# 4-bit feed-forward: two constants leave the vector engine's passes, and two quantisations are interleaved except for groups 0, 1 and 7

## The reference, cut to what matters

```
def fp4_quant_dequant(x):                      # BLOCK = 16
    xb = x.reshape(shape[:-1] + (shape[-1] // BLOCK, BLOCK))
    scale = jnp.maximum(jnp.max(jnp.abs(xb), axis=-1, keepdims=True) / 6.0, 1e-12)
    xn = xb / scale
    idx = jnp.searchsorted(_MID, jnp.abs(xn))
    q = _GRID[idx] * jnp.sign(xn) * scale
    return q.reshape(shape)
def fp4_linear(x, w):
    return jnp.einsum('bsk,nk->bsn', fp4_quant_dequant(x), fp4_quant_dequant(w))

gate = fp4_linear(x, w_gate)                   # 128 -> 352
y = fp4_linear(x, w_up)                        # 128 -> 352
h = silu(gate) * y
return fp4_linear(h, w_down)                   # 352 -> 128
...
x = x + 0.5 * _L3_ffn_ref(_layernorm(x, axis=-1), ...)      # layer 10 and layer 12
```

## Time and profile before

| | |
|---|---|
| median of 3 runs | 4637.05 us (4632.97 to 4646.21) |
| the profiled execution's own time | 4633.54 us |
| its span, first to last instruction | 4631.7 us |
| busy over the span | PE 86%, DVE 75%, ACT 66%, POOL 33% |
| granted TensorE clock, mean | 0.925 of full speed |
| first 4-bit stage | about 3547 to 3729 us of the span |
| second 4-bit stage | about 4438 us to the end |

### The profile page before, as it was taken

How to read it: one execution, slowest core, us unless ns; L and a number is a source line. 1 busy time by engine, 2 the same in 40 slices (tenths; PEclk the granted TensorE clock), 3 DMA queues, 4 the chain that set the end, 5 groups by cost and what they waited for, 6 DMA issues and landing times.

```text
span 4631.7 us, 66074 instructions
## 1 busy us (share of the span) xinstructions
PE 3976.3 (86%) x15980; PEld 2217.0 (48%) x15980; DVE 3491.4 (75%) x11277; ACT 3068.7 (66%) x5649; POOL 1524.9 (33%) x2846
## 2 busy tenths in 40 slices
PE   5688759999999999999999999984978659999965
PEld 4466624444444444444444444432555437676644
DVE  6888489888788788787887887866657946665578
ACT  3455239999899899898998999971222226555532
POOL 2222134444444444444444444433000023333310
PEclk8788779999999999999999999996998779999987
DMA  2122010000000000000000000000000001111100
GB/s 56 28 40 30 15 23 1 8 17 1 20 5 1 22 3 8 17 1 20 5 1 22 3 13 12 1 1 0 1 0 0 0 28 42 41 39 36 40 1 18
DMA packets 148935, 71.87 MB, mean 16 GB/s; under 512 B 109241, under 2 KB 141710, under 8 KB 146212
## 3 DMA queue, kind: packets, MB, share of 16 engines
q1 hardware_dynamic: 140916, 54.72, 5.1%
q10 hardware_dynamic: 7600, 12.58, 0.7%
HBM read 54.48 MB, written 12.80 MB: 15 GB/s over the span
## 4 chain that ended last, share of the span: by engine, by line
PE 54%; DVE 20%; ACT 12%; issue 8%; DMA 4%; POOL 1%; ACTq 1%; DVEq 0%; SPq 0%; POOLq 0%
PE bank L1877 18%; PE bank L1892 6%; PE bank L1921 5%; PE bank L2653 4%; DMA packed_dram<-arena 3%; PE bank L1931 3%; DVE arena L1324 2%; PE bank L655 2%; PE bank L2686 2%; DVE arena L1328 2%; ACT arena L1969 2%; ACT arena L1968 2%; ACT L2015 2%; ACT arena L1981 2%; ACT arena L1972 2%
## 5 line engine op out<-in xcount | busy, mean ns | idle before, releaser
L1877 PE MATMUL bank<-arena 128*128 128x512 f32 x3072 | 1421.3, 596 | 12.3 <-issue 6.0
L1877 PEld LDWEIGHTS bank<-arena 128*128 128x128 f32 x3072 | 585.9, 191 | 755.0 <-issue 730.3
L2118 POOL TENSOR_SCALAR arena<-arena 128x256 f32<-128x256 f32 x1024 | 483.2, 483 | 1187.7 <-DVE arena L2051 1187.7
L1892 PE MATMUL bank<-arena 128*128 128x512 f32 x1024 | 525.0, 604 | 63.3 <-DVE arena L2081 62.9
L2040 DVE SCALAR_TENSOR_TENSOR arena<-arena 128x256 f32<-128x256 f32 x1024 | 393.5, 421 | 181.7 <-ACT arena L1969 173.8
L2081 DVE SCALAR_TENSOR_TENSOR arena<-arena 128x256 f32<-128x256 f32 x1024 | 493.0, 525 | 13.7 <-issue 12.6
L2058 DVE SCALAR_TENSOR_TENSOR arena<-bank,bv,arena 128x256 f32<-128x256 f32 x1024 | 444.7, 472 | 0.0
L1968 ACT ACTIVATE arena<-bank,bqk 128x512 f32<-128x512 f32 x512 | 348.3, 680 | 76.7 <-PE bank L1877 68.2
L2051 DVE SCALAR_TENSOR_TENSOR arena<-bank,bq,arena 128x512 f32<-128x512 f32 x512 | 384.1, 750 | 18.0
L1981 ACT ACTIVATE arena<-arena,const_table 128x512 f32<-128x512 f32 x512 | 374.6, 732 | 0.0
L2664 DVE TENSOR_REDUCE arena<-bank 128x2 f32<-128x512 f32 x256 | 176.4, 689 | 252.3 <-PE bank L2655 252.2
(11 more groups left out here) (370 smaller groups left out, 7498.9 us busy)
## 6 DMA issues: line engine op xcount, KB each, us to landing
arena<-packed_dram SPq DMA_DIRECT2D x48, 192.0 KB
arena<-packed_dram ACTq DMA_DIRECT2D x16, 576.0 KB
arena<-diag_dram SPq DMA_DIRECT2D x16, 256.0 KB, 3.9
arena<-in_L_attn_Wk_dram SPq DMA_DIRECT2D x16, 256.0 KB, 3.3
arena<-in_L_attn_Wq_dram SPq DMA_DIRECT2D x16, 256.0 KB, 4.0
arena<-in_L_attn_Wv_dram SPq DMA_DIRECT2D x16, 256.0 KB, 4.3
arena<-in_L_attn_Wo_dram SPq DMA_DIRECT2D x8, 512.0 KB, 3.8
arena<-in_L_attn_W_dram SPq DMA_DIRECT2D x16, 256.0 KB, 3.4
```

The source lines that it names most:

```text
L1877: nc.tensor.matmul(bank[:, RING1[m % 5], :], w1p[k][:, i * P:(i + 1) * P], zT_of(g), start=True, stop=True).then_inc(a1_proj.sem, 1)
L1892: nc.tensor.matmul(bank[:, 6, :], wo1[:, i, :], a1_att[:, i % 4, :], start=(i == 0), stop=(i == NB1 - 1)).then_inc(a1_outd.sem, 1)
L2118: last = nc.gpsimd.tensor_scalar(a, a, 1.0, a1_ksum[:, i % 4, b:b + 1], ALU.add, ALU.mult)
```

## The change

Two things are done to the activations' quantisations of the 4-bit stage; the weights keep the ten passes.

1. The pass L723 (clamp and multiply) leaves DVE. ACT multiplies m by the magic constant (`magic_x_act`, 128x512; `magic_h_act`, 128x1408), and the clamp moves into the two passes behind it, which become scalar_tensor_tensor with `max` as their first operation. The sign that this turns round is put right in the last pass. So a quantisation is a head of six DVE passes, one ACT multiplication, and a tail of three DVE passes.
2. On DVE, x(g)'s tail moves behind h(g-1)'s head, and h(g-1)'s tail behind x(g)'s tail, for groups 2 to 6. For groups 0, 1 and 7 x(g)'s tail stays directly behind its head. x gets scratch tiles of its own, since both quantisations are now open at once. The wait for the buffer of h (`f3_turned.wait_free`) moves to the tail of h.

```
+        FP4_HEAD = 6
+        FP4_MAGIC = 1.5 * 2.0 ** 22
+        def fp4_tail(dst, scale, v, m, nb):
+            blocks = lambda a: a.rearrange("p (n k) -> p n k", k=BLOCK)
+            return [
+                lambda: nc.vector.scalar_tensor_tensor(v, m, FP4_MAGIC, v, ALU.max, ALU.add),
+                lambda: nc.vector.scalar_tensor_tensor(v, m, FP4_MAGIC, v, ALU.max, ALU.subtract),
+                lambda: nc.vector.scalar_tensor_tensor(blocks(dst), blocks(v), -1.0,
+                                                       scale.unsqueeze(2).to_broadcast([P, nb, BLOCK]),
+                                                       ALU.mult, ALU.mult),
+            ]
...
             def quant_x_dve(g, u):
...
-                for i, step in enumerate(steps):
+                steps = fp4_steps(..., f3_xs[:], f3_xi[:], f3_xv[:], f3_xm[:], NBX)[:FP4_HEAD]
...
+            def alone(g):
+                return isinstance(g, int) and g in (0, 1, G - 1)
+            def round_x_dve(g, u):
+                if not alone(g):
+                    finish_x_dve(g, u)
+            def quant_x_alone_dve(g, u):
+                quant_x_dve(g, u)
+                if alone(g):
+                    finish_x_dve(g, u)
+            def finish_x_dve(g, u):
+                s = g + rep * G
+                dst = f3_xq[:, u, :, :].rearrange("p q d -> p (q d)")
+                f3_magic["x"].wait(nc.vector, s)
+                for i, step in enumerate(fp4_tail(dst, f3_xs[:], f3_xv[:], f3_xm[:], NBX)):
+                    step().then_inc(f3_xstep.sem, 1)
+                    f3_xstep.wait(nc.vector, s, FP4_HEAD + i + 1)
+            def early_act(g, u):
+                if alone(g):
+                    copy_act(g, u)
+                    silu_act(g, u)
+            def late_act(g, u):
+                if not alone(g):
+                    copy_act(g, u)
+                    silu_act(g, u)
+            def magic_x_act(g, u):
+                f3_xstep.wait(nc.scalar, s, FP4_HEAD)
+                nc.scalar.activation(f3_xm[:], f3_xm[:], ACT.Copy, scale=FP4_MAGIC).then_inc(f3_magic["x"].sem, 1)
+            def magic_h_act(g, u):
+                f3_hstep.wait(nc.scalar, s, FP4_HEAD)
+                nc.scalar.activation(f3_m[:], f3_m[:], ACT.Copy, scale=FP4_MAGIC).then_inc(f3_magic["h"].sem, 1)
...
+            def round_h_dve(g, u):
+                f3_magic["h"].wait(nc.vector, s)
+                f3_turned.wait_free(nc.vector, s)
+                for i, step in enumerate(fp4_tail(dst, f3_scale[:], f3_v[:], f3_m[:], NBH)):
+                    step().then_inc(f3_hstep.sem, 1)
+                    f3_hstep.wait(nc.vector, s, FP4_HEAD + i + 1)
...
-                e, [(0, stats_dve), (1, apply_dve), (1, quant_x_dve), (2, quant_h_dve), (3, add_dve)]))
+                e, [(0, stats_dve), (1, apply_dve), (1, quant_x_alone_dve), (2, quant_h_dve), (1, round_x_dve),
+                    (2, round_h_dve), (3, add_dve)]))
...
-                e, [(0, copy_act), (0, silu_act), (1, copy_h_act)], gate(e, n)))
+                e, [(0, magic_x_act), (0, early_act), (1, magic_h_act), (0, late_act), (1, copy_h_act)], gate(e, n)))
```

More of the change, by code:

```diff
@@ L749, in macaron @@
             f3_h = scratch("f3_h", [P, QT, FF3])
+            NBX = QT * D // BLOCK
+            f3_xs = scratch("f3_xs", [P, NBX])
+            f3_xi = scratch("f3_xi", [P, NBX])
+            f3_xv = scratch("f3_xv", [P, QT * D])
+            f3_xm = scratch("f3_xm", [P, QT * D])
             f3_silu = scratch("f3_silu", [P, 2, QT, FF3])
@@ L755, in macaron @@
             f3_wstep = sem("f3_wstep")
-            f3_xstep = ev("f3_xstep", per=FP4_STEPS)
-            f3_hstep = ev("f3_hstep", per=FP4_STEPS)
+            f3_xstep = ev("f3_xstep", per=FP4_STEPS - 1)
+            f3_hstep = ev("f3_hstep", per=FP4_STEPS - 1)
+            f3_magic = {}
             f3_up = ev("f3_up", per=QT)
@@ L781, in ffn3 @@
             stats_dve, rstd_pool, apply_dve, _, copy_act = ln_steps(n, 1e-5)
+            if not rep:
+                f3_magic.update(x=ev("f3_xmagic", after="a0_out"), h=ev("f3_hmagic", after="a0_ocopied"))
             def quant_x_dve(g, u):
@@ L785, in quant_x_dve @@
                 ln_applied.wait(nc.vector, g + n * G)
[L786 to L789, removed]
+                dst = f3_xq[:, u, :, :].rearrange("p q d -> p (q d)")
+                steps = fp4_steps(xn[:, u, :, :].rearrange("p q d -> p (q d)"), dst, f3_xs[:], f3_xi[:],
+                                  f3_xv[:], f3_xm[:], NBX)[:FP4_HEAD]
                 for i, step in enumerate(steps):
@@ L828, in quant_h_dve @@
                 f3_mul.wait(nc.vector, s)
[L829 to L832, removed]
+                dst = f3_hq[:, u, :, :].rearrange("p q f -> p (q f)")
+                steps = fp4_steps(f3_h[:].rearrange("p q f -> p (q f)"), dst, f3_scale[:], f3_inv[:],
+                                  f3_v[:], f3_m[:], NBH)[:FP4_HEAD]
                 for i, step in enumerate(steps):
```

## The result

Over 20 runs each, the changed kernel takes 4653.47 us in the median (4639.28 to 4673.58), the kernel before 4644.32 (4629.32 to 4655.39). The ratio is 1.0023, 95% interval [1.0013, 1.0034]: slower by 10.7 us on 4644 (6.0 to 15.8 by the interval; the medians themselves lie 9.15 us apart), inside the bound of 0.3% and clear of zero. The forecast was +8.9 us. (Its 4646 us stood on the three runs known then, whose median was 4637.05. On the 20-run median it would be 4653.2.)

What follows compares the result with a forecast made beforehand. DVE was taken to bound the 4-bit stages. Per stage, start +4.9, middle -6.95, extra waits +0.5 and end +6.0 gave +4.45, twice +8.9 on 4637.05: 4646 us, own range 4637 to 4654, 8-in-10 range 4632 to 4658.

Steps and rivals of the forecast that it cites:

- What bounds the stage, and what is removed: 4-bit stages: DVE bounds, busy 20.74 of 22.20 us per middle slot; L723's removal saves 1.39 us per group, 22.2 in all.
- Tail passes at no extra cost, ACT's 1408 columns at 1.38 us, no second table load: Quantisations: scalar_tensor_tensor costs what tensor_tensor does; uncovered ACT multiplications hold DVE 0.8 us for x, 1.53 for h.
- Middle slots hidden: x(2) to x(6) with h(1) to h(5): DVE passes cover ACT's multiplications; five slots save 6.95 us, waits take back 0.5.
- The chain to h's product: Middle slots, x(g)'s end through transposes, ups and silu to h(g)'s product: 7.6 to 9.3 us, hidden under 10.7.
- rival 4: Middle slots: the chain to h(g)'s product becomes the bound from 10.7 us on; 4665 us, or 4655 at half; chance 0.12.
- The start: Start of each stage: x(1)'s multiplication behind silu(0) and h(0)'s behind silu(1) on ACT cost +4.0 to +5.9 us, taken +4.9.
- The end: From h(5)'s end to h(7)'s: late x(7), exposed h(6), group 7's copy behind magic_h(6); +6.0 us per stage, +4.0 to +7.5.
- The sum: Both 4-bit stages: 4.9 - 6.95 + 0.5 + 6.0 = +4.45 us per stage, +8.9 in all, range +2 to +15.
- rival 3: Every slot: all of ACT's multiplications are exposed; +7.5 us per stage, +15 in all, 4652 us; chance 0.07.
- 1: Stage edges: only the multiplications' own length is exposed, ACT's queue delays nobody; -8 us in all, 4629 us; chance 0.10.
- 2: Both 4-bit stages: the removed passes' full price is gained, -22.2 us, 4615 us; chance 0.05.
- 5: ACT in each stage: an extra table load before the new Copy, 1.28 us a stage, +2.6, 4648.5 us; chance 0.06.

Runs made afterwards that it cites:

- e6: Changed kernel's order on DVE, but DVE does every multiplication of m itself, ACT none: ratio 0.9993 to the kernel before.
- e5: Changed kernel, but ACT multiplies only for x(2) to x(6) and h(1) to h(5), DVE for the six others: ratio 0.9983 to the kernel before.
- e1: Changed kernel, but ACT multiplies for x(1) between the second and third silu pair of group 0: ratio 1.0007 to the kernel before.
- e9: Changed kernel plus four 128x352 copies on ACT ahead of each group's last copy, making the chain 1.44 us longer: ratio 1.0055 to the kernel before.
- e10: Changed kernel plus eight 128x352 copies on ACT ahead of each group's last copy, making the chain 2.9 us longer: ratio 1.0105 to the kernel before.
- e3: Changed kernel, but ACT's list has lags 2 and 3, so copy and silu of group 7 precede magic_h(6): ratio 1.0007 to the kernel before.
- e2: Changed kernel without exceptions, x(0), x(1) and x(7) interleaved as well on DVE and ACT: ratio 0.9997 to the kernel before.
- e8: Changed kernel, but ACT makes a second 128x1408 pass ahead of h's multiplication for groups 1 to 6: ratio 1.0030 to the kernel before.

## Why the prediction was right, step by step

- **What bounds the stage, and what is removed.** Right. DVE was the bound; e6 and e5 differ only in who multiplies in ten places, and the middle differs by 5.9 and 6.7 us against 5 x 1.39 = 6.95 less 0.5.
- **Tail passes at no extra cost, ACT's 1408 columns at 1.38 us, no second table load.** 1625 and 693 ns, 1377 ns, one load. The hand-overs too: a bare multiplication held DVE for 0.77 and 1.50 us where 0.8 and 1.53 were taken.
- **Middle slots hidden.** -6.38 and -6.84 us against -6.45. The forecast took the two stages as alike within 0.1 us; but the middle of the kernel before differs by 0.70 us between them and that of the changed one by 0.24, and the 0.46 between these is why the gains differ.
- **The chain to h's product.** The spare time came out near the forecast, 1.42 to 1.87 us against 1.4, by two errors that cancel. The chain took 9.45 to 9.68 us, past the forecast's bound of 9.3, and what lies over it took 11.1 to 11.4, not 10.7. In e1 the same chain is 10.5 to 10.7 us, with 0.4 to 0.8 us left. e9 and e10 put the threshold between 11.0 and 11.75 us, so rival 4's mechanism is real, its 10.7 was too low, and it stayed out by about 1.4 us.
- **The start.** +5.4 and +5.3 us against +4.9. h(0)'s product came 3.3 us later than in the kernel before (4487.86 - 4468.76 = 19.10 from x(0)'s first pass, before 15.76), where 3.1 was forecast; e1 shows that the order on ACT did it. The wait before h(0)'s tail was 2.96, in the forecast's span of 1.9 to 3.7. The wait before x(1)'s tail was 6.15 us. The forecast's list of signs says 3.7 there, which its own working contradicts: x(1)'s head was to end at 4452.3 (L722's end in the trace before, 4452.0, and 0.3) and its tail to start at 4458.2, 5.9 us later.
- **The end.** +6.65 and +6.4 us against +6.0. Counted from h(5)'s end, x(7)'s multiplication started at 6.0 us (6.5 forecast) and group 7's copy at 17.3 (17.95); the wait before h(7)'s product was 3.63, not 2.6, because silu(7) took 9.45 us from its copy (4622.18 to 4631.63), longer than the 8.3 chosen and than the bound of 9.1, with the clock at 0.64. The copy was 0.65 us early and silu(7) 1.15 us long: the +0.5 that is left is the difference of two errors. e3 removes this wait, so the lists' different view of group 7 was its cause.
- **The sum.** +5.69 and +4.92 us a stage, 10.6, against +8.9; the times say 10.7. Both edge terms were taken 0.4 to 0.65 too small. In the end term the ups explain it: they ran mostly at 1.2 GHz, and the 8.3 us that I chose for copy to silu was 9.45. The start term missed by 0.2 us in h(0)'s product and by 0.3 in silu(1), which ended 8.73 us after x(1) where about 8.4 was taken. The absolute time, 4653.47 us, lies only 0.5 inside the forecast's own range of 4637 to 4654; that is no error of the terms but the kernel before's own median, 4644.32 over 20 runs where three had given 4637.05. The interval of the times (+6.0 to +15.8) would also admit rival 3's +15; what rules it out is the middle slots.
- **Rivals.** 1 is refuted by e1 and e3, 2 by the result, 3 by the middle slots without a wait for ACT, 5 by the single load. The rule of the Trainium skill ("ScalarE: Activation LUTs", section "Rules for kernel authors"), that a multiplication belongs on VectorE, agrees with the six edge places and disagrees with the ten of the middle: e5, which follows it only at the edges, has shorter stages than the kernel before and the changed one. The same page of the Trainium skill, section "What ACT_TABLE_LOAD costs", has 186 + 0.833 ns a column with immediates, by estimate 1359 ns for 1408 columns, where 1377 were measured.

## What to carry to other kernels

A pass moved to another engine was gained only where the first engine had other work at that moment, and what it cost elsewhere was set by what stood ahead of it in the other engine's program, not by its length alone: here 1.5 us cost up to 3, and 0.8 up to 6. In a pipeline over groups, look at first and last slots separately and let them do the work the old way; the middle gained 6.6 us a stage, the edges lost 11.9.
When an exception is written on a group's number, check for every engine that the number is a number there: a list with a shorter lag has that group in its loop, and the exception silently does not hold.
When runs scatter by 0.5% and the change moves 0.2%, measure stretches between fixed instructions of the stage; here most of them repeat within 0.4 us.

## What I had not expected of the hardware

The last group's matmuls, 24 of them at the very end of the kernel, took 5.49 us in the trace before and 2.94 in the one after. A window over them in each, the kernel before first:

```profile
4617.50:4623.00 5.50, 5.49 (x24) 5.20 (x24) 0.00 (x0) 0.00 (x0) 0.00 (x0) 0.50 0.00 0
```

```profile
4649.60:4652.60 3.00, 2.93 (x24) 2.75 (x24) 0.00 (x0) 0.01 (x1) 0.00 (x0) 1.00 0.00 0
```

The clock is at 1.2 GHz in the one and at 2.4 in the other, after transposes of 2.92 us and a pause before them, 7.14 us in the kernel before and 9.62 in the changed one. The pause's length does not decide it: in e1 and e2 it is 9.62 us too, with the same transposes, and the last matmuls took 5.43 and 5.49; in e8, again after 9.62, they took 2.94. What decides it is not shown here. From h(7)'s end to the last add's start it is 9.9 to 10.0 us in five of the twelve traces, 7.5 in three, and between these in four. 2.5 us of a kernel's time can thus lie in the clock of its last burst, more than several of the terms above. The forecast's "what follows h(7) is unchanged" was off by 2.6 us in this pair of traces, by this alone. Why layer 11 takes 720 us in one execution and 740 in another, with the same instructions, was not looked into and stays open.
